# Edge softmax of a graph network: the multiply of numerator and inverse denominator on GpSimd in place of VectorE

## What is computed

```
w_m = (efeat @ W_msg  + b_msg ).reshape(E, 16, 16)
w_a = (efeat @ W_attn + b_attn).reshape(E, 16, 16)
h   = feat[src][:, :, None]
e1, e2 = w_m * h, w_a * h
seg_max = segment_max(e2, dst)
ex    = exp(e2 - seg_max[dst])
denom = segment_sum(ex, dst)
ft    = segment_sum(e1 * ex / denom[dst], dst)
return ft.sum(axis=1)
```

## Time and profile before

| | |
|---|---|
| median of 3 runs | 6274.11 us (6266.36 to 6280.92) |
| the profiled execution | 6263.25 us, of which the span of its instructions 6261.1 us |
| VectorE busy over the span | 3572.3 us, 57% |
| TensorE busy | 3220.7 us, 51% |
| GpSimd busy | 3165.4 us, 51% |
| ScalarE busy | 1639.0 us, 26% |

### The profile page before, as it was taken

The page is one execution under the profiler, slowest core; times in us unless marked ns, Lnnn a source line. Parts: engine busy times, 40 slices in busy tenths (PEclk is TensorE's granted clock), DMA queues, the critical chain, the costliest instruction groups (busy, mean ns, idle before and its releaser), DMA issues. The chain is left out here.

```text
span 6261.1 us, 56658 instructions
## 1 busy us (share of the span) xinstructions
PE 3220.7 (51%) x12357; PEld 2379.2 (38%) x12357; DVE 3572.3 (57%) x6225; ACT 1639.0 (26%) x4111; POOL 3165.4 (51%) x2659
## 2 busy tenths in 40 slices
PE   5888888884344443997000355000454300077776
PEld 2444444442344443886000353000453200077642
DVE  6899899897755552887111583010687400066678
ACT  2555555553311111444000112000112200022234
POOL 3666666664088887887777101777000377600000
PEclk9999999999755555998555668555666555566688
DMA  2111111112244432211000003000002100000012
GB/s 81 43 40 41 42 38 43 40 38 57 80 59 60 59 56 38 59 47 48 7 6 6 1 0 90 7 6 6 1 0 79 47 7 6 5 1 1 1 50 62
DMA packets 394890, 212.24 MB, mean 34 GB/s; under 512 B 126954, under 2 KB 364974, under 8 KB 394754
## 3 DMA queue, kind: packets, MB, share of 16 engines
q1 hardware_dynamic: 275474, 191.16, 10.8%
q0 software_dynamic: 119296, 19.68, 5.3%
HBM read 152.10 MB, written 58.54 MB: 34 GB/s over the span
## 5 line engine op out<-in xcount | busy, mean ns | idle before, releaser
L1108 PE MATMUL ps<-arena 128*128 128x128 f32 x2976 | 639.9, 399 | 1461.2 <-DVE arena L1545 775.7
L677 POOL DMA_INDIRECT extra<-x_t,srci x784 | 800.4, 1021 | 794.9 <-issue 794.9
L1108 PEld LDWEIGHTS ps<-arena 128*128 128x128 f32 x2976 | 591.7, 303 | 1498.3 <-issue 1492.1
L1536 DVE TENSOR_TENSOR arena<-ps,relp 128x1024 f32<-128x1024 f32 x186 | 226.7, 1219 | 974.7 <-remote 901.3
L662 POOL DMA_INDIRECT sums<-cmb,sidx x392 | 613.4, 1565 | 330.4 <-ACT cmb L795 198.7
L1013 PE MATMUL ps<-edge_in,wl 17*128 17x512 f32 x784 | 704.4, 1076 | 133.2 <-DMA edge_in<-far_row 131.1
L677 POOL DMA_INDIRECT extra<-h_t,srci x392 | 396.2, 1011 | 527.4 <-issue 527.4
L640 POOL DMA_INDIRECT xg<-in_x,xidx x392 | 438.0, 1117 | 376.9 <-DVE xp L1334 257.2
L851 ACT ACTIVATE ps<-extra 128x16 f32 x1488 | 176.3, 170 | 1613.9 <-DVE arena L1545 1021.6
L629 POOL DMA_INDIRECT ft_t<-fts,fidx x392 | 509.2, 1299 | 141.3 <-issue 117.9
L1562 DVE TENSOR_TENSOR arena<-arena,ps 128x128 f32 x1488 | 426.6, 287 | 231.7 <-issue 59.3
(11 more groups left out here) (197 smaller groups left out, 6064.6 us busy)
## 6 DMA issues: line engine op xcount, KB each, us to landing
edge_in<-far_row SPq DMA_DIRECT2D x98, 256.0 KB
ain<-in_src_row SPq DMA_DIRECT2D x56, 448.0 KB
sums<-zero SPq DMA_DIRECT2D x132, 144.0 KB
arena<-rel_t SPq DMA_DIRECT2D x63, 256.0 KB
x_t<-yout SPq DMA_DIRECT2D x28, 448.0 KB, 3.3
xin<-x_t SPq DMA_DIRECT2D x28, 448.0 KB, 4.3
extra<-x_t,srci POOLq DMA_INDIRECT x784
ain<-x_t SPq DMA_DIRECT2D x28, 448.0 KB, 4.7
```

The lines of the kernel that those rows point to most:

```text
L677: pool.indirect_dma_start(dy[:, t, :], None, table, bass.IndirectOffsetOnAxis(ap=srci[:, t:t + 1], axis=0)).then_inc(d_gathered[n % QUEUE] ...
L1108: last = pe.matmul(slot_sums(k, n)[:, j * P:(j + 1) * P], oneh[b][:, j * P:(j + 1) * P], placed[b][:, j * P:(j + 1) * P], start=True, stop ...
```

## The change

VectorE no longer does L1384. GpSimd does the same product, now as a plain multiply, as the last thing in its step n, for tile n-3, behind the gather (in odd steps) and the scatter. The factor `inv` gets a second buffer, in the unused tile `extra`. ScalarE's wait before it writes `inv` moves back one tile with it. VectorE gets a new wait: before the scan that writes `num` of tile m it waits until the product of tile m-2 is done, since `num` has two buffers and another engine now reads them.

```diff
-        hS, ww, lnd, inv = halves[0:4]
+        hS, ww, lnd = halves[0:3]
+        inv = [halves[3], extra[:, 0:UNIT].rearrange("p (h e) -> p h e", h=CH)]
...
@@ gpsimd, step(i, c), behind the four scatters
+                ratio(i, c - 3)
+
+            def ratio(i, c):
+                if not inside(i, c, TILES):
+                    return
+                b = c % 2
+                pool.wait_ge(inv_done, 2 * i + c + 1)
+                pool.wait_ge(num_done, 2 * i + c + 1)
+                if later(i, c, 2):
+                    pool.wait_ge(ft_ps, 2 * i + c - 1)
+                pool.tensor_tensor(rat[b], body(num[b]), inv[b], ALU.mult).then_inc(rat_done, 1)
...
@@ scalar, step(i, c)
-                    if later(i, c - 2, 1):
-                        act.wait_ge(rat_done, 2 * i + c - 2)
-                    act.activation(inv[:, :, :], lnd[:, :, :], ACT.Exp, scale=-1.0).then_inc(inv_done, 1)
+                    if later(i, c - 2, 2):
+                        act.wait_ge(rat_done, 2 * i + c - 3)
+                    act.activation(inv[b], lnd[:, :, :], ACT.Exp, scale=-1.0).then_inc(inv_done, 1)
...
@@ vector, step(i, c)
+                    if later(i, c - 1, 2):
+                        dve.wait_ge(rat_done, m - 1)
                     dve.tensor_tensor_scan(num[o], dd[o], qq, 0.0, ALU.mult, ALU.add).then_inc(num_done, 1)
-                if inside(i, c - 2, TILES):
-
-                    m = n - 2
-                    dve.wait_ge(inv_done, m + 1)
-                    if later(i, c - 2, 2):
-                        dve.wait_ge(ft_ps, m - 1)
-                    dve.wait_ge(num_done, m + 1)
-                    dve.scalar_tensor_tensor(rat[b], body(num[b]), 1.0, inv, ALU.mult, ALU.mult).then_inc(rat_done, 1)
```

## The result

The changed kernel takes 6826.52 us (median of 4 runs, 6824.79 to 6832.53), the kernel before 6277.23 us in the same four rounds. The ratio is 1.0869, 95% interval 1.0856 to 1.0882: 549 us slower. The forecast was 6820 us, with a range of 6750 to 6940.

The account below looks back on a forecast made before the run. A loop through POOL, SP, PE and DVE, little longer than DVE's work, bounds the stage at 29.07 us per pair; a new closed loop of 41.1 adds 548 us, the tail 1, giving 6820 us, range 6750 to 6940.

Parts of the forecast that it names:

- The loop: Softmax stage: split, gather, scatter, product, PE, one DVE step, split form a closed chain, 41.1 us per pair against 29.07.
- e2: DVE's instruction at L1346 in the softmax stage, which waits for PE's L1013; PE's path to it forecast at 8.4 us.
- The product: POOL's 128x1024 multiply, behind gathers and scatters in odd steps: 2.5 us, bounds 1.20 and 4.27.
- One slow gather: On POOL in odd steps, one of eight gathers stays slow beside a DVE scan; the eight take 11.0 us.
- The hidden steps: The pair's other product, DVE's new wait before num, SP's loads and ScalarE's inv wait cost nothing beside the PE path.
- The even product: POOL's product in even steps: done 28.6 us after the gather's start, before PE can read it at 31.
- The drain: Stage tail, last e2 to last scatter: 41 to 43 us against 39.7; net +1 us, within -3 and +6.
- The total: Whole kernel: stage +548 us and tail +1 us, giving 6820 us.
- PE's clock: More idling of PE can't slow its matmuls, which already run at the lower of two clock levels.
- Rival A: Product ready within 4.5 us of the gather's start, so hidden; DVE's 109 us gained, 6165 us; chance 5%.
- Rival B: Queues overlap and only POOL's own work bounds the pair: 33.1 us, +185 us, 6460 us; chance 8%.
- Rival C: POOL's products or DMAs disturb each other: product 4.27, gathers 12.94, pair 44.8 us, 6990 us; chance 12%.

Follow-up runs that it names:

- the same kernel as the first: The changed kernel with the gather put last in POOL's odd steps, behind scatter and product: 5247.21 us, ratio 1.0119 to the kernel before.

## Why the prediction was right, point by point

- **The loop.** Right in every link, and in which waits come and go. Its terms, as forecast and as in the timeline above: split to gather 2.21 and 2.19; gathers 11.0 and 11.07; scatters 5.13 and 4.86; product with release 2.6 and 2.32; PE to e2 8.4 and 8.36; the DVE step 11.75 and 11.76. Sum 41.1 and 40.56.
- **The product** was the term most off: 2.18 us, not 2.5. Twice the half-size row was too much: a line through the two sizes (1.27 and 2.18) leaves an estimate of 0.36 us that doesn't grow with the size. The estimate that I set beside it from the Trainium skill (GPSIMD Engine Reference, Elementwise — side-by-side cycle accounting, which gives 4497 ns for 2048 values), 2.25, was the better one; this row is near it.

```profile
L642 POOL TENSOR_TENSOR arena<-arena x49: 2174/2182/2207, 122.1 to 2026.8; 128x1024 f32<-128x1024 f32 x49
```

- **One slow gather.** Right: of the eight, seven take 0.95 to 1.00 and one 1.84.
- **The hidden steps.** DVE's new wait for POOL is 9.5 us per pair in `num` (10 forecast) and costs nothing, as e2 waits another 6.0 for PE behind it. The even product has 4.2 us to spare, and doubling it confirmed this. POOL's wait for the split is longer than forecast, 14.4 us and not 12: POOL is through with both steps 26.2 us after the gather's start, where I had 28.6.
- **The drain** was mis-sized: the last e2 is at 2002.24 and POOL's last scatter over at 2046.24, 44.0 us against the 39.7 of before, where I had reckoned 41 to 43, and DVE's lead came to nothing. From the last split to the end it is 71.4 in place of 66.5, +4.9 for my +1 (inside the bounds I gave). DVE's L1380 lost 2.0 us twice there to POOL's product, a collision that I had priced only in the other direction. One of the two:

```profile
2008.33 2.19 POOL L642 TENSOR_TENSOR arena<-arena,extra 128x1024 f32<-128x1024 f32 x1
2008.35 3.26 DVE L1380 SCALAR_TENSOR_TENSOR arena<-arena 128x1024 f32<-128x1024 f32 x1
```

- **The total** is nearer than the terms deserve. In the traces the stage grew by 528 and the drain by 5: 533, where I had 549. The measured difference of the medians is 549. So my terms were 16 us too high, and something that I hadn't priced made up for it; that is luck. Where it lies isn't shown: the two profiled executions differ by 570, of it 36 behind the stage, but the one before was faster than its median by 14 and the one after slower by 6, and the stage of the kernel before itself varies by 31 us between two traces.
- **PE's clock** did no harm: the eight matmuls of L1025 (L1013 before) take 7.19 us in both kernels.
- **Rival A** (product hidden) fell, and its deciding point was right: it comes true when the product no longer stands behind the gather, but then POOL's queue takes over. **Rival B** (33.1 us, POOL's own work) had the right mechanism for the opened loop, with 29.4 for my 33.1. Most of the error is the split's 2.21 us: POOL doesn't wait for it there, so it isn't in its queue. In the pair from 815.48 to 845.31 of the kernel with the product first, the gathers fill 12.9 us (12.94 forecast), the scatters 12.3 (12.9) and the products 4.7 (5.0). **Rival C** did not occur: the 98 products take 2.17 to 2.21 us, and the eight gathers 11.07.

## What to carry to other kernels

In these kernels a queue gives what it makes last only when all before it is through, and that includes what the items before it wait for (16.2 us for PE's sum). Before moving work onto a half idle queue, follow its consumer back: if consumer, queue and the wait at the head of the queue close a loop, the time of the loop is the price, not the work. The wait at the head can perhaps go behind the items that don't need it; that reordering alone was worth 65 us here, and on top of it, moving half of the multiplies lost 37 of them and moving all lost 128.

## What the runs showed of the hardware that I had not expected

- POOL's multiply and a DVE instruction with two SBUF inputs hold each other: on DVE 128x1024 took 2.66 to 3.90 us in place of 1.22, a scan 3.70 in place of 2.27, a 128x128 subtraction 3.00 in place of 0.29. On POOL the 128x896 multiply took 2.81 in place of 1.69. The rows before the change showed only POOL being held. The Trainium skill (Advanced Engine Details and Errata, GPSIMD Details) states that POOL shares a read and a write interface with DVE and conflicts with DVE instructions that have two SBUF inputs; these rows agree, and both engines pay.
- By the recorded starts, a DVE instruction that starts 0.6 us ahead of the multiply is still held to 1.1 us behind its end (835.09 and 835.71 above). The subtraction at 505.59 would even have been over at 505.88, ahead of the product's start at 506.24. In the same kernel as the first, an L1380 that starts 0.75 us ahead (1457.23) takes its 1.22, and there the product takes 2.52. So, by an estimate from these rows, who is held is settled some 0.7 us ahead of the start that POOL's row shows; what happens in that time they don't show.
- The granted clock is given as 1.00 through the softmax stage of all kernels, while its matmuls have the durations of the lower of the two levels: 0.90 us for 512 columns, where a later layer takes 0.226 for 256 at a granted 1.00. In the kernel before, the granted clock first differs from 1.00 behind the stage (0.94 between 1600 and 1640 us).
- The same program took 6277 us in one session and 5183 to 5187 in three others, on three chips. The difference lies almost all behind the softmax stage; its cause stays open.
